# A delta-rule block on one core: output products placed between the products with the inverse, and two element-wise steps given to ScalarE

## The chip, the cores and the metric

The kernel runs on one core of a Trainium2 chip. The metric is the time of one execution on the device in microseconds (us). Before the change the median of 3 runs is 2594.55 us (2590.03 to 2601.16). TensorE does matrix products, VectorE and ScalarE work on rows of elements, GpSimd (POOL in the rows) does small and slow element-wise work, and SyncE (SP) issues DMAs. The engines run beside each other and wait on semaphores.

## The reference

For 2 x 4096 tokens of width 512 the reference adds three things: the input, an attention block and a feed-forward block, both on the layer-normalised input. Cut to what is computed:

```python
xn = layernorm(x)                                   # eps 1e-5
q, k = l2n(heads(xn @ Wq)) * dh**-0.5, l2n(heads(xn @ Wk))   # 16 heads of 32
v, beta = heads(silu(xn @ Wv)), sigmoid(xn @ Wb)
# for each token t, batch and head: S is 32 x 32
#   delta = (v_t - S^T k_t) * beta_t ;  S = S + k_t delta^T ;  o_t = S^T q_t
o = o * rsqrt(mean(o*o) + 1e-5) * o_norm_weight
attn = o @ Wo
ffn = ((silu((xn @ fp8(gate_w)) * gate_scale)) * ((xn @ fp8(up_w)) * up_scale)) @ fp8(down_w) * down_scale
out = x + attn + ffn
```

## The kernel before

**Tiling.** The 4096 tokens of each batch are cut into 16 spans of 256. One span holds both batches: 512 tokens, 4 tiles of 128, and 8 chunks of 32 tokens per batch and head. The recurrence is solved chunk by chunk: for each of 256 problems (2 batches, 16 heads, 8 chunks) a 32 x 32 triangular system is inverted, and the state is then carried over the 8 chunks in turn.

**A span on TensorE**, in the order in which it is issued. (1) Projections: 13 jobs, each a group of 128 output columns, 12 products of 128 x 512 (8 for the beta projection, JOB_B), from the high and low halves of the normalised input and the weights. Between them stand eight groups of Gram products (`gram(g)`, 8 x 4 problems each), K^T K and K^T Q: pairs 0-1 after job 4, 2-3 after job 5, 4 to 7 together after job 8. (2) The output products of the previous span, `project_out(j)` for 4 tiles, 12 products each, jobs 13 to 16. (3) Gate and up products, 24 halves of 8. (4) Eight groups of small products with the inverse (`quads` at L450, the UW products): they give W and U of each problem. Group g writes PSUM bank T[g % 4], so group 4 must wait until group 0 is read. (5) The state chain, 8 chunks c: products with the state, 6 products of the down projection (`down`), then, in some chunks, the transposes of the next span's normalised input (XT_AT), products that update the state, and 6 more down products. All small products are on 32 x 32 tiles of the array and go through the helper `quads` (L306).

**VectorE.** It reads projections, sums squares, reads the Gram results (`read_grams`, L956 transposes them, L958 masks the K^T Q half, L962 multiplies by beta), and solves all systems at once: 62 operations in turn (`row_products` L1020, `off_rows` L1027), each needing the one before. Other work is put between them by operation number: V_AT (transposes of V from PSUM), OUT_AT (`add_out`, adding an output product to the result), VK_AT (`values_by_k`, L1054, one operation that scales V by the norm of k), FUSE_AT (`fuse_tile`: the low part of the last tile, L1003, and gate times up, L1013). `fuse_tile(10)` and `(11)` stand behind the first and second half's transpose of the inverse (`t_transposed`, L1037). After this come `read_w`, the statistics of the next span's input, and in the chain a read, a subtraction, a read and an addition per chunk.

**ScalarE** evacuates projections, computes silu and tanh, makes the high parts, copies U (`copy_u`, L605) and the chain's outputs. **GpSimd** zeroes the matrix of the inverse, does the square roots by Newton steps, and adds the down products. **SyncE** stores a span's result once its four output tiles are added (`wo_added`) and then loads the span after next into the same buffer.

**Order and banks.** Every engine's order is written out by hand. Dense jobs use the PSUM banks D[job % 4]; `take(job)` waits until job - 4 has been read. `tt` holds the transposed inverse with the 32 columns of a problem side by side; it is what TensorE loads as weights in step 4. The output in high and low parts lives in the last four tiles of f_hi and f_lo. The loop's body holds two spans (`two_spans`); two spans stand ahead of the loop, which goes round 7 times.

## Time and profile before

| | |
|---|---|
| median of 3 runs | 2594.55 us |
| profiled execution, its time | 2598.04 us |
| its span, first to last instruction | 2596.3 us |
| mean granted TensorE clock | 0.98 |
| TensorE busy | 2290.9 us, 88% |
| VectorE busy | 1932.2 us, 74% |
| ScalarE busy | 661.6 us, 25% |
| GpSimd busy | 315.2 us, 12% |

The profile is one execution. A line names the engine, the line of the kernel, the operation, the tile written and the tiles read, and how many there are. `128*128` or `32*32` behind an operation on TensorE (PE) is the part of the array; a 32-bit product on a small tile is two instructions, each with its own weight load (PEld). Mean durations of pipelined instructions overlap: what one costs in a row of equals is the distance between starts. A bracket at the end of a line is the idle time of the engine before it and what ended that time; "issue" means that nothing in the profile ended it.

### The profile page before, as it was taken

Reading aid. Unit: us, or ns where it says so; the run is one execution under the profiler, and the core shown is the slowest. Engines: PE = TensorE matmul, PEld = TensorE weight load, DVE = VectorE, ACT = ScalarE, POOL = GpSimd, SP = SyncE. Lnnn points to the kernel's source line nnn. Section 1 sums busy time; section 2 is a strip of 40 time slices with the busy share of each in tenths; the row PEclk is TensorE's granted clock in tenths of the full one; section 3 lists DMA queues with packets and bytes.
Section 4 is the critical chain, followed back from the end, with each engine's and each line's share of the span. In section 5 each row is a group of like instructions: output and inputs, shape, how many; then the busy total and the mean of one; then the engine's idle time right before and its main releaser. Section 6 shows DMA issues by size and latency. Waiting matters only on the chain.

```text
span 2596.3 us, 92717 instructions
## 1 busy us (share of the span) xinstructions
PE 2290.9 (88%) x40736; PEld 1286.9 (50%) x40992; DVE 1932.2 (74%) x3291; ACT 661.6 (25%) x1110; POOL 315.2 (12%) x528
## 2 busy tenths in 40 slices
PE   0198999989899998989989899998989899898996
PEld 0045545455554545455454555545554454545543
DVE  7986685958768596776959587695967769496785
ACT  2123222213222222222222222222222222122221
POOL 4510101001010100102010010201001020100200
PEclk9999999999999999999999999999999999999998
DMA  5100010000001000000000000010100100000010
GB/s 170 61 18 2 3 34 4 33 3 19 18 3 34 3 34 3 17 20 3 34 4 34 3 13 24 3 34 3 34 3 3 34 3 34 4 34 3 2 34 18
DMA packets 27184, 54.56 MB, mean 21 GB/s; under 512 B 5152, under 2 KB 5152, under 8 KB 26784
## 3 DMA queue, kind: packets, MB, share of 16 engines
q1 hardware_dynamic: 26784, 48.55, 5.5%
q8 instruction: 334, 5.47, 0.9%
q14 instruction: 66, 0.54, 0.1%
HBM read 31.76 MB, written 16.78 MB: 19 GB/s over the span
## 4 chain that ended last, share of the span: by engine, by line
PE 88%; issue 6%; DVE 4%; DMA 0%; ACT 0%; POOL 0%; SPq 0%; DVEq 0%
PE D L380 21%; PE T L306 21%; PE D L391 13%; PE D L390 13%; PE D L462 8%; PE D L321 7%; PE D L461 4%; PE D L311 1%; DVE kq L227 1%; DVE at L781 0%; DVE f_lo L780 0%; DVE w_lo L822 0%; DVE stats L744 0%; DVE wgu L233 0%; DVE kq L1042 0%
## 5 line engine op out<-in xcount | busy, mean ns | idle before, releaser
L390 PE MATMUL D<-xt_hi,wgu 128*128 128x512 f16 x1536 | 582.1, 379 | 0.0
L391 PE MATMUL D<-xt_lo,wgu 128*128 128x512 f16 x1536 | 582.1, 379 | 0.0
L462 PE MATMUL D<-wd,f_lo 128*128 128x512 bf16 x768 | 297.0, 387 | 43.1 <-issue 43.1
L380 PE MATMUL D<-xt_hi,w_hi 128*128 128x512 f16 x832 | 319.3, 384 | 12.9 <-issue 12.9
L380 PE MATMUL D<-xt_lo,w_hi 128*128 128x512 f16 x832 | 318.4, 383 | 0.0
L380 PE MATMUL D<-xt_hi,w_lo 128*128 128x512 f16 x768 | 293.9, 383 | 0.0
L598 ACT ACTIVATE sg<-D,gs 128x512 f32<-128x512 f32 x192 | 132.0, 687 | 573.6 <-PE D L391 573.6
L1027 DVE TENSOR_TENSOR at<-at,outer_v 128x62 f32<-128x62 f32 (+15 forms) x496 | 259.3, 523 | 12.1
L1020 DVE TENSOR_TENSOR outer_v<-mt,at 128x62 f32<-128x62 f32 (+15 forms) x496 | 258.2, 521 | 11.6
L391 PEld LDWEIGHTS D<-xt_lo,wgu 128*128 128x128 f16 x1536 | 150.3, 98 | 181.2
L390 PEld LDWEIGHTS D<-xt_hi,wgu 128*128 128x128 f16 x1536 | 150.3, 98 | 181.2
L1113 DVE STREAM_TRANSPOSE outer_p<-T 128x256 f32<-128x256 f32 x128 | 57.6, 450 | 193.4 <-PE T L306 193.4
L461 PE MATMUL D<-wd,f_hi 128*128 128x512 bf16 x512 | 198.2, 387 | 0.0
L306 PE MATMUL T<-kpv,mt 32*32 32x64 f32 x8192 | 136.3, 222 | 67.5 <-issue 67.5
L306 PE MATMUL T<-kq,state 32*32 32x64 f32 x8192 | 155.3, 221 | 24.7 <-ACT kpv L605 18.9
L306 PEld LDWEIGHTS T<-kq,state 32*32 32x32 f32 x8192 | 130.0, 108 | 79.0 <-issue 78.7
L306 PEld LDWEIGHTS T<-kpv,mt 32*32 32x32 f32 x8192 | 126.7, 110 | 81.0 <-issue 81.0
L726 POOL TENSOR_TENSOR rstd<-var_e,neg_half 128x4 f32<-128x4 f32 x16 | 16.4, 1026 | 1222.9 <-DVE var_e L1105 1222.9
L1093 DVE STREAM_TRANSPOSE outer_v<-T 128x256 f32<-128x256 f32 x128 | 57.6, 450 | 143.0 <-PE T L306 143.0
L306 PE MATMUL T<-kpv 32*32 32x64 f32 x8192 | 148.2, 219 | 3.4 <-issue 2.7
L732 POOL TENSOR_TENSOR xs<-xs,fuse 128x512 f32<-128x512 f32 x64 | 81.1, 1267 | 575.8 <-DVE fuse L1087 575.8
L306 PEld LDWEIGHTS T<-kpv 32*32 32x32 f32 x8192 | 125.4, 107 | 46.1 <-issue 45.9
(153 smaller groups left out, 3314.0 us busy)
## 6 DMA issues: line engine op xcount, KB each, us to landing
xs<-_attn_hidden_states_dram SPq DMA_DIRECT2D x34, 512.0 KB, 4.2
out_dram<-xs SPq DMA_DIRECT2D x32, 512.0 KB, 3.3
f_hi<-in_L_ffn_down_w_dram SPq DMA_DIRECT2D x4, 768.0 KB, 4.5
kq<-in_L_ffn_gate_w_dram SPq DMA_DIRECT2D x3, 768.0 KB, 4.4
f_hi<-in_L_ffn_up_w_dram SPq DMA_DIRECT2D x2, 768.0 KB, 6.2
kq<-in_L_ffn_up_w_dram SPq DMA_DIRECT2D x2, 768.0 KB, 6.6
qt<-in_L_attn_Wq_dram SPq DMA_DIRECT2D x1, 1024.0 KB, 8.1
kpv<-in_L_attn_Wk_dram SPq DMA_DIRECT2D x1, 1024.0 KB, 10.4
```

The lines of the kernel that those rows point to most:

```text
L306: last = nc.tensor.matmul(out[s], lhs[s], rhs[s], start=start, stop=True, skip_group_check=shared)
L321: ins = nc.tensor.matmul(D[bank][:, :], o_part[:, m, j * P:(j + 1) * P], w[:, m, :], start=n == 0, stop=n == 3 * MS - 1)
L380: last = nc.tensor.matmul(D[bank][:, :], w[:, k, cols], xp[:, k, :], start=n == 0, stop=n == len(parts) * KT_ - 1)
L390: nc.tensor.matmul(D[bank][:, :], wgu[:, k, c:c + P], xt_hi[:, k, :], start=k == 0, stop=False)
L391: last = nc.tensor.matmul(D[bank][:, :], wgu[:, k, c:c + P], xt_lo[:, k, :], start=False, stop=k == KT_ - 1)
L461: nc.tensor.matmul(D[bank][:, :], f_hi[:, ic, j * P:(j + 1) * P], wd[:, ic, :], start=ic == 0, stop=False)
L462: last = nc.tensor.matmul(D[bank][:, :], f_lo[:, ic, j * P:(j + 1) * P], wd[:, ic, :], start=False, stop=ic == IC - 1)
L598: nc.scalar.activation(sg[:, ic % 2, :], D[bank_of(gate_up_job(2 * ic))][:, :], ACT.Silu, scale=gs[:, ic:ic + 1]).then_inc(sg_ready, 1)
L732: nc.gpsimd.tensor_tensor(xs[:, par, j, :], xs[:, par, j, :], fuse[:, j % 2, :], ALU.add).then_inc(acc_ready, 1)
L1020: solved[0] = step(nc.vector.tensor_tensor(products(j), m_prob[:, :, j, j + 1:].unsqueeze(3).to_broadcast(shape), t_prob[:, :, j, 0:j + 1] ...
L1027: solved[0] = step(nc.vector.tensor_tensor(rest, rest, products(j), ALU.subtract))
L1093: nc.vector.transpose(blocks(outer_v), chain_banks(c)[:, :, :, 0, :]).then_inc(ws_read, 1)
```

## The change

It makes these edits at once.

- **Order on TensorE.** The beta projection moves from job 2 to job 5. Output products of tiles 2 and 3 leave their place before gate-up and become jobs 39 and 40: half a tile (6 products) stands behind inverse groups 1, 3, 5 and 7. Job 8 and the first 4 products of job 9 stand between Gram pairs 4-5 and 6-7.
- **ScalarE.** It masks the K^T Q half of the second 32 problems, 32 calls over one column each, and scales V by the norm of k, 64 calls of 32 elements (8 behind each of the gate silus 2 to 9). VectorE's operations for these two are gone (the mask of the first half stays).
- **VectorE.** All twelve `fuse_tile` stand inside the solve; output additions 2 and 3 move behind inverse reads 4 and 7. The statistics of the next span's input go batch by batch: the first before the chain, the second in chunk 2, with the aggregation in chunks 0 and 3 and the normalisation in chunks 1 and 4; the input's transposes are in chunks 2, 3, 5 and 6. Some steps of the reading stage change their order.
- **Layout.** `tt` keeps the problem number innermost, so that `t_transposed` writes in order and TensorE loads its weights at a step of 32 elements.
- **Buffers.** The normalised output goes into `at` and its high and low parts into the memory of `qt`; f_hi and f_lo are used so by the last span alone. GpSimd zeroes `at` after the low part is made, behind its first Newton steps.
- **Loads and stores** go batch by batch, each with its semaphore.
- **Loop.** Four spans per turn, four ahead of it, 3 turns.

```diff
-JOB_K, JOB_B, JOB_Q, JOB_V, JOB_WO, JOB_GU, JOB_DN = (0, 3, 5, 7), 2, (1, 4, 6, 8), (9, 10, 11, 12), 13, 17, 41
+JOB_K, JOB_B, JOB_Q, JOB_V, JOB_WO, JOB_GU, JOB_DN = (0, 2, 4, 7), 5, (1, 3, 6, 8), (9, 10, 11, 12), (13, 14, 39, 40), 15, 41
-XT_AT = {2: 0, 3: 1, 4: 2, 5: 3}
+XT_AT = {2: 0, 3: 1, 5: 2, 6: 3}
-V_AT = {0: 0, 4: 1, 9: 2, 13: 3}
-OUT_AT = {17: 0, 20: 1, 22: 2, 25: 3}
-VK_AT = 23
-FUSE_AT = {27: 0, 31: 1, 34: 2, 37: 3, 40: 4, 43: 5, 46: 6, 50: 7, 54: 8, 60: 9}
+V_AT = {0: 0, 2: 1, 7: 2, 12: 3}
+OUT_AT = {16: 0, 18: 1}
+VK_AT = {ic: range(8 * (ic - 2), 8 * (ic - 1)) for ic in range(2, 10)}
+FUSE_AT = {20: 0, 24: 1, 27: 2, 30: 3, 33: 4, 36: 5, 39: 6, 42: 7, 45: 8, 49: 9, 53: 10, 58: 11}
+STATS_AT, AGGREGATE_AT, APPLY_AT = {2: 1}, {0: 0, 3: 1}, {1: 0, 4: 1}
...
-        tt = mt[:, :].rearrange("p (n t) -> p n t", t=CHUNK)
+        tt = mt[:, :].rearrange("p (g t n) -> p g t n", g=2, t=CHUNK)
...
-                    project(5)
+                    project(JOB_B)
                     gram(2)
                     gram(3)
                     project(6)
                     project(7)
-                    project(8)
                     gram(4)
                     gram(5)
+                    project(8)
+                    project(9, end=4)
                     gram(6)
                     gram(7)
-                    for job in range(9, PROJECTIONS):
+                    project(9, first=4)
+                    for job in range(10, PROJECTIONS):
                         project(job)
 
                     pe.wait_ge(olo_ready, since(1, 1))
-                    for j in range(TILES):
-                        project_out(j, take(JOB_WO + j))
+                    for j in range(2):
+                        project_out(j, take(JOB_WO[j]))
...
-                            last = quads(T[g % 4][:, 64 * n:64 * n + 64], tt[:, pc, :], kpv[:, 1:3, pc * DH:(pc + 1) * DH])
+                            last = quads(T[g % 4][:, 64 * n:64 * n + 64], tt[:, pc // 32, :, pc % 32], kpv[:, 1:3, pc * DH:(pc + 1) * DH])
                         last.then_inc(tiled_done, 1)
+                        if g % 2:
+                            j, half = 2 + g // 4, g // 2 % 2
+                            bank = bank_of(JOB_WO[j]) if half else take(JOB_WO[j])
+                            project_out(j, bank, groups=range(2 * half, 2 * half + 2))
...
+                    act.wait_ge(m_ready, since(2, 2))
+                    act.wait_ge(q_read, since(1, 1))
+                    for i in range(CHUNK):
+                        masked = nc.scalar.activation(pt[:, 32:64, i], grams[:, :, 1, i], ACT.Identity, scale=causal[:, i:i + 1])
+                    masked.then_inc(p_ready, 1)
...
+                    def values_by_k(n):
+
+                        v_problem = vt[:, n, :]
+                        return nc.scalar.activation(v_problem, v_problem, ACT.Identity, scale=rk[:, n:n + 1])
...
                     for ic in range(IC):
                         silu_gate(ic)
+                        if ic in VK_AT:
+                            if VK_AT[ic][0] == 0:
+                                act.wait_ge(v_ready, since(MS, MS))
+                                act.wait_ge(k_norm_ready, since(1, 1))
+                            for n in VK_AT[ic]:
+                                scaled = values_by_k(n)
...
-                        nc.vector.transpose(tt[:, 32 * s:32 * s + 32, :].rearrange("p n t -> p t n"), t_prob[:, s]).then_inc(tt_ready, 1)
+                        nc.vector.transpose(tt[:, s], t_prob[:, s]).then_inc(tt_ready, 1)
...
                     t_transposed(0)
-                    fuse_tile(10)
                     t_transposed(1)
-                    fuse_tile(11)
-
-                    dve.wait_ge(x_loaded, since(32, 64))
-                    dve.nop(nofuse=True)
+
                     for g in range(8):
                         read_w(g)
                         if g == 1:
                             low_part(IC - 1)
-                        if g > 3:
-                            step(layer_norm_stats(g - 4, 1 - par))
+                        if g == 4:
+                            add_out(2)
+                    read_statistics(0)
+                    add_out(3)
...
-            with dve.Fori(1, SPANS // 2) as it:
-                two_spans(it)
+            with dve.Fori(1, SPANS // TURNS) as it:
+                some_spans(it)
```

## Rows read from the trace of the kernel before

**Rows 1.** The page: the chain that ended last, by engine.

```profile
PE 88%; issue 6%; DVE 4%; DMA 0%; ACT 0%; POOL 0%; SPq 0%; DVEq 0%
```

**Rows 2.** The chain in order of time: start, length (us), engine, tile, line.

```profile
282.89 12.09 PE D L380 x56
...
1040.42 2.16 issue
1042.59 13.94 PE D L380 x56
...
1166.72 0.44 PE D L311 x4
...
1196.32 12.09 PE D L380 x56
...
1222.84 2.68 PE T L306 x178
...
1228.12 10.47 PE D L380 x48
1238.58 10.36 PE D L321 x48
...
2565.95 2.49 DVE sso L1142 x4
```

**Rows 3.** TensorE's timeline, inverse products of two spans: start, us, operation.

```profile
1138.26 2.56 PE L306 MATMUL T<-kpv,mt 32*32 32x64 f32 x168
1142.17 1.98 PE L306 MATMUL T<-kpv,mt 32*32 32x64 f32 x126 [1.36 <-issue]
1146.10 3.59 PE L306 MATMUL T<-kpv,mt 32*32 32x64 f32 x126 [1.95 <-issue]
...
1152.83 0.71 PE L306 MATMUL T<-kq,state 32*32 32x64 f32 x34 [1.19 <-ACT kpv L605]
...
1290.31 3.88 PE L306 MATMUL T<-kpv,mt 32*32 32x64 f32 x261
1296.04 5.47 PE L306 MATMUL T<-kpv,mt 32*32 32x64 f32 x251 [1.85 <-issue]
1302.71 0.21 PE L306 MATMUL T<-kq,state 32*32 32x64 f32 x1 [1.20 <-ACT kpv L605]
```

**Rows 4.** TensorE's timeline in the chain, two half-steps.

```profile
1161.79 1.10 PE L306 MATMUL T<-kpv 32*32 32x64 f32 x64
...
1164.22 1.10 PE L306 MATMUL T<-kq,state 32*32 32x64 f32 x64
```

**Rows 5.** Windows: stretch, length, TensorE busy (matmuls), granted clock, DMA share, GB/s.

```profile
1147.00:1148.00 1.00, 1.00 (x49) 0.50 0.08 16
```

**Rows 6.** VectorE's timeline, from the second half's Gram results to the inverse's transpose.

```profile
1228.17 1.25 DVE L956 STREAM_TRANSPOSE mt<-T 128x1024 f32<-128x1024 f32 x1 [2.35 <-PE T L306]
...
1232.37 0.17 DVE L1020 TENSOR_TENSOR outer_v<-mt,at 128x62 f32<-128x62 f32 x1
...
1247.62 2.29 DVE L1054 TENSOR_TENSOR kpv<-kpv,rk 128x2048 f32<-128x2048 f32 x1
...
1269.86 0.69 DVE L1003 TENSOR_TENSOR f_lo<-fuse,f_hi 128x512 f16<-128x512 f32 x1 [0.23 <-PE D L391]
1270.47 0.74 DVE L1013 SCALAR_TENSOR_TENSOR fuse<-D,usf,sg 128x512 f32<-128x512 f32 x1
...
1283.08 0.28 DVE L1020 TENSOR_TENSOR outer_v<-mt,at 128x120 f32<-128x120 f32 x1
...
1285.45 1.97 DVE L1037 STREAM_TRANSPOSE mt<-at 128x1024 f32<-128x1024 f32 x1
```

**Rows 7.** Groups of ScalarE by line: count, busy us, mean ns, idle before.

```profile
L592 ACT ACTIVATE f_hi<-fuse 128x512 f16<-128x512 f32 x192 | 119.3, 621 | 32.7 <-DVE fuse L1013 32.7
...
L574 ACT ACTIVATE tb<-tb,w_inv 128x64 f32<-128x64 f32 x16 | 5.6, 348 | 26.3 <-DVE tb L923 26.3
...
L616 ACT ACTIVATE wd<-wd,row_inv 128x512 bf16<-128x512 bf16 x12 | 7.4, 706 | 0.0
```

More of the change, by code:

```diff
@@ L312, in transpose_xn, with project_out @@
                 last.then_inc(dense_done, 1)
[L314 to L317 removed]
+            def project_out(j, bank, last=False, groups=range(MS)):
+                hi, lo = (last_hi, last_lo) if last else (o_hi, o_lo)
+                for m in groups:
                     if last:
                         pe.wait_ge(olo_ready, SPANS + m + 1)
[L320 removed]
+                    for n, (o_part, w) in enumerate(((hi, wo_hi), (lo, wo_hi), (hi, wo_lo))):
                         ins = nc.tensor.matmul(D[bank][:, :], o_part[:, m, j * P:(j + 1) * P], w[:, m, :],
[L322 to L324 removed]
+                                                start=m == 0 and n == 0, stop=m == MS - 1 and n == 2)
+                if MS - 1 in groups:
+                    ins.then_inc(dense_done, 1)
             pe.wait_ge(consts, 2)
@@ L370, in take, with project @@
                         return bank_of(job)
-                    def project(job):
-                        bank = take(job)
-                        group = (4, 0, 12, 5, 1, 6, 2, 7, 3, 8, 9, 10, 11)[job]
+                    def project(job, first=0, end=12):
+                        bank = bank_of(job) if first else take(job)
+                        group = (4, 0, 5, 1, 6, 12, 2, 7, 3, 8, 9, 10, 11)[job]
                         cols = slice(group * P, (group + 1) * P)
                         parts = ((w_hi, xt_hi), (w_hi, xt_lo), (w_lo, xt_hi))[:2 if job == JOB_B else 3]
-                        n = 0
-                        for k in range(KT_):
-                            for w, xp in parts:
-                                last = nc.tensor.matmul(D[bank][:, :], w[:, k, cols], xp[:, k, :],
-                                                        start=n == 0, stop=n == len(parts) * KT_ - 1)
-                                n += 1
-                        last.then_inc(dense_done, 1)
+                        products = [(k, w, xp) for k in range(KT_) for w, xp in parts]
+                        for n in range(first, min(end, len(products))):
+                            k, w, xp = products[n]
+                            last = nc.tensor.matmul(D[bank][:, :], w[:, k, cols], xp[:, k, :],
+                                                    start=n == 0, stop=n == len(products) - 1)
+                        if n == len(products) - 1:
+                            last.then_inc(dense_done, 1)
                     def gate_up(half):
@@ L760, in one @@
                 dve.wait_ge(set_v, done[0])
[L763 removed]
+            for b in range(BATCH):
+                dve.wait_ge(x_loaded[b], 16)
             for j in range(TILES):
@@ L980, in two_spans @@
                     k_to_tokens(1)
-                    beta_over_k(0)
-                    o_scale(it, par, after, step)
-                    if first and par == 0:
+                    q_sum(1)
+                    o_scale(it, turn, after, step)
+                    if first and turn == 0:
                         gate_up_scale()
-                    q_sum(1)
-                    read_grams(0)
                     k_sum(2)
+                    b_to_tokens()
                     k_to_tokens(2)
                     o_low()
+                    read_grams(0)
+                    beta_over_k(0)
+                    times_beta(0)
                     q_sum(2)
```

235 lines of the change are left out of this document (127 added, 108 removed).

## The prediction

> **What bounds the kernel now.** I read the page's chain first: 88% of the chain that ended last is TensorE, and another 6% is "issue", time in which the engine waited for nothing that the profile shows [rows 1]. So the span is TensorE's content plus its holes, and the question is where the holes are. The chain in order of time gives the beats [rows 2]: the kernel does 16 spans of tokens, and from the start of the second (282.89) to the end of the sixteenth (2565.95) is 2283.1 us, 152.2 for each of 15. The content of one: 48 output products took 10.36 us, 0.216 each [rows 2]; a group of small products (64 matmul instructions) takes 0.95 us, as 261 of them took 3.88 [rows 3]; in the state chain a half-step of 64 small and 6 dense instructions repeats every 2.43 us [rows 4], which is 0.96 + 1.30 + 0.17 for the crossing between kinds. A span has 392 dense products outside the chain (84.6 us), 16 small groups outside it (15.4), 16 half-steps (38.9) and 4 transposes of 0.44 (1.8) [rows 2]: 140.7 us. So 11.5 us of each span are holes or slow clock.
>
> They lie in four places. (a) The last four groups of Gram products run 1222.84 to 1228.12, 5.3 us for 3.9: 1.4 us. (b) The products with the inverse: 14.6 us from 1138.26 to 1152.83 and 12.4 from 1290.31 to 1302.71 (seven spans are like the one, eight like the other), for a content of 7.7 [rows 3]. The stalls fall inside groups and are "issue": from 1142.17 there are 126 matmuls in 1.98 us and then 1.95 of nothing. I read this as TensorE eating small instructions faster than they arrive: 126 matmuls with their weight loads are 252 instructions in 3.9 us when starved, 65 per us, against 135 per us wanted. The dense work wants 9, so it refills. (c) The chain wants 58 per us, just under the supply, but starts empty; what is left of 11.5 after the rest is about 2.7 us. (d) Back-edges of the loop: 2.2 us idle at 1040.42, then 13.94 us for what takes 12.09 in the next span [rows 2]; there are six of them, and as three show hardly any slow stretch I price one at 3.2 us. The slow stretch is the clock: 0.50 was granted (1.2 GHz of 2.4) in 1147 to 1148 after a 1.95 us stall [rows 5]. At the low level 49 small instructions pass per us; a dense product costs double.
>
> **The change, part by part.**
>
> *Less ahead of the inverse products.* Output products 2 and 3 (24 dense, 5.18 us) leave the stretch between V projections and gate-up. Eight products of the beta projection now stand between Gram pairs 0-3, and 16 dense ones between pairs 4-5 and 6-7. Two pairs at 65 per us of supply then never run dry: hole (a) goes, 1.4, for one more crossing, 0.17. From the start of a span gate-up ended at 94.0 (1290.31 [rows 3] less 1196.32 [rows 2]); now 94.0 - 5.2 - 1.4 + 0.2 = 87.6. For this the first half's read must be in time: an estimate of VectorE's new sequence up to the mask ends at 23.8, and TensorE wants it at 24.1 (60 + 8 + 24 dense products and four groups). I take no stall, with up to 1 us as a bound.
>
> *The tail of the solve.* This is where part of it is lost. All twelve fuse_tile calls stand inside the 62 solve operations now, the last before operation 58. It cannot start before the last gate-up product ends, and TensorE's next work needs the inverse's transpose, which comes behind it. So TensorE stands still for: 0.2 latency, the low part 0.6 (1269.86 to 1270.47), the fused product 0.7, operations 58 to 61 1.1 us (1283.08 to 1285.45 less a low part and a fused product that stood between them), and the transpose, 1.25 [rows 6]. The transpose wrote with a 128-byte step, 1.97 us for 1024 elements; written in place it should cost as the one of Gram results, 1.25. Sum 3.85 us, until 91.5. Before, the first transpose (1285.45) was done when gate-up ended. Is VectorE there in time? The solve ran from 1232.37 to 1285.45, 53.1 us with 4 V transposes less one, 4 output additions, 10 fused tiles, 9 low parts and the scaling of the values (2.2). New: less 2.2 and 1.3 for two additions, plus 2.5 for two more tiles with low parts and 0.6 for the first V transpose; it starts at 34.2 (masking half two on VectorE, 1.2, is gone), which would end it at 87; the products pace it instead. So the tail is real and no longer.
>
> After 3.85 us of idleness the clock will fall as it did after 1.95. Here the price is 0.66 us for the first two groups (128 at 49 per us are 2.6, not 1.9) and up to 1 for dense work: bounds 0 and 1.7, I take 0.8.
>
> *Inverse products with output products between.* 8 groups (7.7) + 24 dense (5.18) + 4 crossings (0.66) = 13.5 us, wanting 1072 instructions; a full buffer had 336 to 522 (the 168 or 261 pairs before the first stall [rows 3]) and 65 per us come in addition, about 880. Enough, so no stalls. Reads by VectorE and copies by ScalarE run under the dense pieces, and the last piece, 1.5 us, hides the last read and copy, where TensorE waited 1.2 before [rows 3]. Chain begins at 91.5 + 13.5 + 0.8 = 105.8; before it was 110.2 (1152.83 less 1042.59) and 106.4.
>
> *Chain.* It starts with about 250 instructions in stock, so I take 1.2 of the 2.7 us of holes (bounds 0.3 and 2.7). Statistics for the second batch move into step 2: with the low part and read_down VectorE is 2.5 us busy, 0.9 late for the next product, which the transpose's 0.44 and 1.3 of dense work just cover; without that cover 0.4 us. Output addition 3 and two statistics (1.9 us) stand ahead of the first read, under that product. The second batch's output additions end at about 106 instead of 56, and SyncE's store and load of that batch are queued behind them; the statistics want the load at about 121, and I take 15 us for a store and a load as enough, at nothing.
>
> *ScalarE.* It takes 32 masking calls of 32 columns and 64 scalings of 32 columns. Its cost per call, bounded by the rows: 64 columns took 0.35 with its wait, and 512 columns 0.62 of which 0.43 are the columns' [rows 7]: 0.17 to 0.35. I take 0.25. Masking: 5 to 11 us, starting at 33 and wanted by the values' silu only, whose results are wanted after 52: hidden. Nothing else of ScalarE is queued behind them until gate-up's first silu at 48. Scaling: 8 per gate-up pair, 1.4 to 2.8 us, where ScalarE has 2.2 of 3.45 free (16 dense products, less a silu and a high part of 0.62 each); at 0.28 it fits. At 0.35 it would be 0.5 late in each of eight pairs, 4 us a span. I take nothing.
>
> *Unrolling by four.* The loop's body holds four spans and four stand ahead of it, so it goes round three times: two back-edges instead of six: 4 x 3.2 = 12.6 us.
>
> *First span.* ScalarE rescales wd for 7.4 us [rows 7] ahead of its first copy, and TensorE's fifth inverse group waits for that copy. Now the standstill (3.8) and two dense pieces stand ahead of that group and cover it: 8 us with the stalls of that span (bounds 3 and 10).
>
> *Strided weights.* The inverse is now stored so that TensorE loads 32 columns at a 128-byte step, 512 loads a span. No row shows TensorE reading so. The nearest is VectorE's write at that step: 0.72 us more for 1024 elements [rows 6], 0.7 ns each, 22 ns a load; four tiles at once and a stream that is paced by instructions (15 ns a pair now) may hide all of it. Bounds 0 and 8192 x 22 ns = 184 us; I take 0, since a pair has 5 ns to spare per tile against what its columns need at 2.4 GHz, 20 per tile of four.
> The Trainium skill speaks against this edit: SBUF — State Buffer, section "Door 1: The DMA port swizzle", says that lines of SBUF are 16 bytes and that each access which crosses into a new line pays a penalty, free steps ending at 4 fp32 values. By it every element of these loads would pay; the transpose's 1.97 against 1.25 us agrees for VectorE's writes, and no row here shows it for TensorE.
>
> **Sum.** A span: 105.8 + 38.9 + 1.8 + 1.2 = 147.7 us, 15 of them and two edges: 2221.8, against 2283.1, a gain of 61.3. With 8 for the first span 69 us off a span of 2596.3: 2527, and with the 1.7 us around it (2598.04) 2529. The profiled execution was 3.5 us above the median of the runs, so a median may come out that much lower.
>
> **Rivals.**
> *Instructions still run dry* (0.17). For it: the 65 per us are an average; the chain wants 58 all the time. Then 1.5 in the chain and 1 in the inverse products come back, 37 us: 2566.
> *Strided weights cost a part* (0.13). If an element took four times as long, a load of 13 ns becomes 53, 20 ns more per four tiles: 128 x 20 ns = 2.6 us a span, 41 us: 2570.
> *Strided weights cost all* (0.08), the slower side. Loads of the four tiles don't overlap: 184 us more, 2713. It decides from 69 us / 8192 = 8.4 ns a load. Against it: loads of 110 ns length pass at 15 ns spacing.
> *The solve becomes the bound* (0.07): the tail or ScalarE's scalings are 4 us later a span, 2593, no change.
> *No slow clock and a full supply in the chain* (0.07): 0.8 and 0.9 us less in each of 16 spans, 27 us: 2502.
> Forecast 0.48. Range 2503 to 2590, the sum's bounds for chain and clock below, the partial rivals above; what is left out is mostly the full strided cost. This kernel's measurement tells 0.5%, 13 us, from no change. Faster 0.78 (the cases under 2581 hold 0.85, less 0.07 for two partial rivals that come together), same 0.11, slower 0.11.
>
> **What would show it.** TensorE idle about 3.9 us before the first inverse product of each span, ended by the inverse's transpose at 1.25 us; inverse products with dense ones in 13.5 to 14.5 us and no mid-group stall; last Gram pairs without stalls; two "issue" gaps of 2.2 us at back-edges; ScalarE's scalings at 0.25 us. Wrong if small products per us fall below 66 in the inverse products at full clock, or if ScalarE's gate silu waits behind scalings.

## The result, and the profile after

The changed kernel took 2602.22 us (median of 20 runs, 2595.02 to 2612.79) against 2594.21 for the kernel before (20 runs): a ratio of 1.003, 95% interval [1.0019, 1.004]. On a second chip it was 2601.68 against 2597.37, 1.0019 [1.0003, 1.0036]. So the time did not change by more than 0.5%, and what little it moved went up. The forecast was 2529, its range 2503 to 2590. The profiled execution took 2603.99 us, its span 2602.3, 75 us over the forecast.

The page of the kernel after, chain that ended last by engine, which answers to [rows 1]:

```profile
PE 89%; DVE 7%; issue 3%; DMA 0%; POOL 0%; ACT 0%; DVEq 0%; SPq 0%
```

"issue" has halved (6% to 3%), as was meant, and VectorE's share has gone from 4% to 7%: a stall on instructions was exchanged for a wait on VectorE. The waits of TensorE name it (line waited for: us in total, times, longest):

```profile
PE T L315 <- DVE mt L1091: 50.5, 12, 4.2
```

They are twelve waits of 4.2 us each, once a span, for the transpose of the inverse. In the first four spans the same pause of 3.9 to 4.0 us is put down to "issue". VectorE's timeline of one span, the seventh, shows what fills it:

```profile
1131.83 0.69 DVE L1057 TENSOR_TENSOR f_lo<-fuse,f_hi 128x512 f16<-128x512 f32 x1
1132.44 0.74 DVE L1067 SCALAR_TENSOR_TENSOR fuse<-D,usf,sg 128x512 f32<-128x512 f32 x1
1133.10 0.27 DVE L1074 TENSOR_TENSOR outer_v<-mt,at 128x120 f32<-128x120 f32 x1
...
1133.98 0.22 DVE L1081 TENSOR_TENSOR at<-at,outer_v 128x62 f32<-128x62 f32 x1
1134.24 2.37 DVE L1091 STREAM_TRANSPOSE mt<-at 128x1024 f32<-128x1024 f32 x2
```

The last fused tile, the last four solve operations and the transpose run one after the other, while TensorE, whose last gate-up product ended at 1131.6, has nothing it may do. TensorE's timeline of the same span (start, us, operation, in brackets the idle time before it), which answers to [rows 3]:

```profile
1131.26 0.38 PE L402 MATMUL D<-xt_lo,wgu 128*128 128x512 f16 x1
1135.83 3.64 PE L315 MATMUL T<-kpv,mt 32*32 32x64 f32 x128 [4.20 <-DVE mt L1091]
1139.41 1.03 PE L330 MATMUL D<-wo_hi,qt 128*128 128x512 f16 x2
...
1142.02 2.10 PE L315 MATMUL T<-kpv,mt 32*32 32x64 f32 x128
1144.06 0.61 PE L330 MATMUL D<-wo_hi,qt 128*128 128x512 f16 x2
...
1145.45 1.76 PE L315 MATMUL T<-kpv,mt 32*32 32x64 f32 x99
...
1150.43 1.16 PE L315 MATMUL T<-kpv,mt 32*32 32x64 f32 x64 [0.32 <-issue]
```

The first 128 small products take 3.58 us (1135.83 to 1139.41), the next 128 take 2.04. The six dense output products between them take 2.61, the next six 1.39. There is no stall inside any of these four pieces: the first two are slow, not interrupted. The last group of the span is interrupted once, for 0.32 us. The windows of this span (stretch, length, TensorE busy with its matmuls, granted clock, DMA share, GB/s), which answer to [rows 5], show why:

```profile
1136.00:1137.00 1.00, 1.00 (x45) 0.50 0.00 0
...
1140.00:1141.00 1.00, 1.00 (x4) 0.50 0.00 0
...
1142.00:1143.00 1.00, 1.00 (x66) 1.00 0.00 0
```

After the pause TensorE is granted 1.2 GHz, not 2.4, for some 6 us of this span, and small and dense products alike cost nearly double.

From the starts of the second to the sixteenth span and of the stretches in them I worked out means for 15 spans (us). The last column is the time at 1.2 GHz in the stretch of the inverse products and in the chain:

| | start to end of gate-up | standstill | inverse stretch | chain to next span | span | at 1.2 GHz in inverse / chain |
|---|---|---|---|---|---|---|
| before | 94.5 | 0 | 13.6 | 44.2 | 152.2 | 1.3 / 3.0 |
| forecast | 87.6 | 3.9 | 14.3 | 41.9 | 147.7 | |
| after | 89.1 | 4.1 | 16.3 | 43.4 | 152.9 | 4.3 / 0 |

The idle time at back-edges lies inside the measured stretches, but not in the forecast's 147.7, which counts two edges apart. So 5.5 us a span were saved ahead of the inverse and 0.8 behind it, and 4.1 and 2.7 were paid between. The balance, 0.7 us a span more (10 us in 15), less the 5 us by which the first span became shorter (159.3 to 154.4), is the 6 us between the two spans (2596.3 and 2602.3), as near as rounded means tell. Of the 16.3 us of the inverse stretch the slow clock took 1.9: in the mean of the 15 spans the first 128 small products and the first six dense ones, the only pieces that meet it, were longer by that than the 2.04 and 1.40 us which such pieces take at 2.4 GHz.

### The profile page after: what moved, and what is told of

Read it like the earlier page. It is cut to its first block, busy times and chain, and to the rows that moved or that the text cites. A ratio compares the mean times of both kernels' runs of the same rounds, so it can differ in the third digit from the quotient of the medians.

```text
span 2602.3 us, 94081 instructions
## 1 busy us (share of the span) xinstructions
PE 2352.2 (90%) x40992; PEld 1293.3 (50%) x40992; DVE 1874.9 (72%) x3275; ACT 968.7 (37%) x2646; POOL 325.3 (13%) x544
## 4 chain that ended last, share of the span: by engine, by line
PE 89%; DVE 7%; issue 3%; DMA 0%; POOL 0%; ACT 0%; DVEq 0%; SPq 0%
PE T L315 22%; PE D L391 21%; PE D L402 13%; PE D L401 13%; PE D L330 7%; PE D L478 7%; PE D L479 6%; PE D L320 1%; DVE kq L233 1%; DVE mt L1091 1%; DVE kpv L1167 1%; DVE at L821 0%; DVE f_lo L820 0%; DVE state L1176 0%; DVE w_lo L862 0%
## 5 line engine op out<-in xcount | busy, mean ns | idle before, releaser
L478 PE MATMUL D<-wd,f_hi 128*128 128x512 bf16 x768 | 293.7, 382 | 1.7 <-issue 1.6
L615 ACT ACTIVATE kpv<-kpv,rk 128x32 f32<-128x32 f32 x1024 | 229.4, 309 | 0.0
L315 PE MATMUL T<-kpv,mt 32*32 32x64 f32 x8192 | 160.6, 238 | 69.7 <-DVE mt L1091 50.5
L766 POOL TENSOR_TENSOR rstd<-var_e,neg_half 128x2 f32<-128x2 f32 x32 | 22.6, 706 | 1487.2 <-DVE var_e L1119 1487.2
L315 PEld LDWEIGHTS T<-kpv,mt 32*32 32x32 f32 x8192 | 148.7, 141 | 101.1 <-issue 100.6
L660 ACT ACTIVATE qt<-T 128x256 f32<-128x256 f32 x128 | 49.2, 384 | 379.3 <-DVE outer_p L1174 379.3
L1096 DVE STREAM_TRANSPOSE kq<-T 128x256 f32<-128x256 f32 x128 | 57.4, 448 | 156.4 <-PE T L315 156.2
L1067 DVE SCALAR_TENSOR_TENSOR fuse<-D,usf,sg 128x512 f32<-128x512 f32 x192 | 143.1, 745 | 26.3 <-PE D L402 26.3
L330 PE MATMUL D<-wo_hi,qt 128*128 128x512 f16 x512 | 160.5, 395 | 1.1 <-issue 1.1
L315 PEld LDWEIGHTS T<-kq,state 32*32 32x32 f32 x8192 | 123.9, 105 | 69.1 <-issue 68.9
```

Of the source, the lines that this page charges most:

```text
L315: last = nc.tensor.matmul(out[s], lhs[s], rhs[s], start=start, stop=True, skip_group_check=shared)
L330: ins = nc.tensor.matmul(D[bank][:, :], o_part[:, m, j * P:(j + 1) * P], w[:, m, :], start=m == 0 and n == 0, stop=m == MS - 1 and n == 2)
L478: nc.tensor.matmul(D[bank][:, :], f_hi[:, ic, j * P:(j + 1) * P], wd[:, ic, :], start=ic == 0, stop=False)
L615: return nc.scalar.activation(v_problem, v_problem, ACT.Identity, scale=rk[:, n:n + 1])
L1067: nc.vector.scalar_tensor_tensor(fuse[:, ic % FUSE_RING, :], D[bank][:, :], usf[:, ic:ic + 1], sg[:, ic % 2, :], ALU.mult, ALU.mult).then_ ...
```

## The experiments

Each comparison is with the kernel before on the same chip; "after" is the changed kernel. The kernel before took 2587.35, 2597.37 and 2590.78 us on the three chips of these runs, so between chips the ratios are compared, not the times.

**Is it the tail?** Theory A: the last fused tiles stand in VectorE's path to the inverse, and the pause makes the clock fall. Its rivals B and C are in the expectation below. A further one, that the small products are slow because of their strided weights, is left to the run on the strided weights. The first run moves both tiles behind the transposes, where they stood before the change.

```diff
-FUSE_AT = {20: 0, 24: 1, 27: 2, 30: 3, 33: 4, 36: 5, 39: 6, 42: 7, 45: 8, 49: 9, 53: 10, 58: 11}
+FUSE_AT = {20: 0, 24: 1, 27: 2, 30: 3, 33: 4, 36: 5, 39: 6, 42: 7, 45: 8, 49: 9}
...
                     t_transposed(0)
+                    fuse_tile(10)
                     t_transposed(1)
+                    fuse_tile(11)
```

> The changed kernel, with fused tiles 10 and 11 behind the first and the second transpose of the inverse, as in the kernel before. Theory A (the standstill ahead of the inverse products is what ate the gain, twice: 4.2 us of idleness and then some 2.8 us because the clock falls to 1.2 GHz behind it): the standstill shrinks to about 1 us, TensorE keeps 2.4 GHz, each span is 5 to 6 us shorter, 16 spans give about 90 us, so about 2510. Theory B (the standstill only fills the instruction supply; without it the same time comes back as stalls inside the small groups): at most 2 us a span, about 2570 to 2600, with issue stalls in the inverse products. Theory C (VectorE is late by itself): the standstill stays above 3 us and the time near 2600.

Measured: 2543.33 us, ratio 0.984 [0.9805, 0.9874]. TensorE's timeline of one span:

```profile
1113.34 2.09 PE L315 MATMUL T<-kpv,mt 32*32 32x64 f32 x128 [1.49 <-DVE mt L1091]
...
1116.76 2.10 PE L315 MATMUL T<-kpv,mt 32*32 32x64 f32 x128
...
1120.19 2.22 PE L315 MATMUL T<-kpv,mt 32*32 32x64 f32 x128
...
1123.74 2.40 PE L315 MATMUL T<-kpv,mt 32*32 32x64 f32 x128
...
1130.26 1.10 PE L315 MATMUL T<-kpv 32*32 32x64 f32 x64
...
1132.69 1.44 PE L315 MATMUL T<-kq,state 32*32 32x64 f32 x64
```

The pause is 1.5 us, the clock falls behind it in none of the 15 spans, and the first 128 products take 2.09 instead of 3.64. A span is 4.0 us shorter. A holds, but its size was too large: 5 to 6 us a span were expected, and the ratio moved by 1.9%, some 49 us (59 between the two traced executions), not 90. The inverse stretch still takes 14.9 us a span where the forecast had 13.5 without slow clock. Its last groups are slower than its first: 2.40 against 2.09 in this span, with no gap that the timeline lists, and in most others with up to 0.6 us of "issue" in a group as well. The stretch without slow clock at 14.9 is only 1.4 us shorter than with it (16.3), though the slow clock costs 1.9: a part, some 0.5 us, came back in the later groups, as theory B has it for the whole. In the chain behind, half-steps of 1.10 us stand beside some of 1.44.

**How long may the pause be?** Only tile 11 moves behind the transpose, tile 10 stays at operation 53.

```diff
-FUSE_AT = {20: 0, 24: 1, 27: 2, 30: 3, 33: 4, 36: 5, 39: 6, 42: 7, 45: 8, 49: 9, 53: 10, 58: 11}
+FUSE_AT = {20: 0, 24: 1, 27: 2, 30: 3, 33: 4, 36: 5, 39: 6, 42: 7, 45: 8, 49: 9, 53: 10}
...
                     t_transposed(0)
+                    fuse_tile(11)
                     t_transposed(1)
```

> The changed kernel, with only fused tile 11 moved behind the first transpose; tile 10 stays inside the solve. A middle dose. Theory A: a standstill of about 2.6 us; if the clock falls as it does after 4.2 us, the gain is the 1.6 us alone, 26 us, about 2575; if it does not fall after so short a pause, 1.6 + 2.8 a span, 70 us, about 2530. Theory B: no gain, 2590 to 2600. Theory C: standstill as before, 2600.

Measured: 2568.9, ratio 0.9933 [0.9911, 0.9953]. Its waits (line waited for: us in total, times, longest):

```profile
PE T L315 <- DVE mt L1091: 33.9, 12, 2.9
```

The pause is 2.8 us, and the clock falls behind it in nine of the 15 spans, a case that the expectation didn't hold. The gain over the kernel after is 1.0%, 25 us, what was expected of the shorter pause alone; the inverse stretch became only 0.7 us shorter (15.5 for 16.3). Three lengths of the same pause thus give three answers: 1.5 us never, 2.8 in nine of 15, 4.2 always.

**The unrolling.** Two spans per turn instead of four, six back-edges instead of two.

```diff
-TURNS = 4
+TURNS = 2
```

> The changed kernel with two spans per turn of the loop instead of four, seven turns: six back-edges instead of two. If a back-edge costs the 3.2 us that I gave it, 13 us more, about 2615. Rival: unrolling by four also placed the instruction stream so that the third span of each turn stalls 3.4 us in the Gram products; two spans per turn lay the stream otherwise, and the time is 2595 to 2605 with the stalls elsewhere or gone.

Measured: 2605.67, ratio 1.0074 [1.0049, 1.0099], 0.44% or 11 us more than the kernel after, and by the two intervals anything from 4 to 18 us. Four back-edges were priced at 12.6 us. The run agrees but does not isolate them, since other terms moved too. In the traces TensorE is idle 1.9 to 2.4 us at each back-edge of either kernel, which is some 9 us for four, and no slow clock follows it in either. The Gram stalls of the 7th, 11th and 15th span are gone in this kernel, which gives back about as much. The chains that end in a back-edge take 46.3 us, 3.5 more than the others, so more than the back-edge lies in them: "issue" stalls inside their small products.

**The strided weights.** The old layout is put back: the transpose writes at a 128-byte step again, and TensorE loads 32 adjacent columns.

```diff
-        tt = mt[:, :].rearrange("p (g t n) -> p g t n", g=2, t=CHUNK)
+        tt = mt[:, :].rearrange("p (n t) -> p n t", t=CHUNK)
...
-                            last = quads(T[g % 4][:, 64 * n:64 * n + 64], tt[:, pc // 32, :, pc % 32], kpv[:, 1:3, pc * DH:(pc + 1) * DH])
+                            last = quads(T[g % 4][:, 64 * n:64 * n + 64], tt[:, pc, :], kpv[:, 1:3, pc * DH:(pc + 1) * DH])
...
-                        nc.vector.transpose(tt[:, s], t_prob[:, s]).then_inc(tt_ready, 1)
+                        nc.vector.transpose(tt[:, 32 * s:32 * s + 32, :].rearrange("p n t -> p t n"), t_prob[:, s]).then_inc(tt_ready, 1)
```

> The changed kernel with the transposed inverse stored as before (32 columns of a problem side by side, VectorE's transpose writing at a 128-byte step). If TensorE loads strided weights at no cost (128 small products and their loads took 1.96 us at 2.4 GHz, 1.90 before), the groups keep their time, and only the standstill grows by 0.7 us with the transpose: about 12 us more, 2614. If strided loads cost, the groups get faster than 1.9 us per 128 and the kernel does not lose: 2590 to 2602.

Measured: 2606.48, ratio 1.0086 [1.0053, 1.012]. TensorE's timeline of one span:

```profile
1136.56 3.63 PE L315 MATMUL T<-kpv,mt 32*32 32x64 f32 x128 [4.87 <-DVE mt L1091]
...
1142.71 2.00 PE L315 MATMUL T<-kpv,mt 32*32 32x64 f32 x128
1144.64 0.60 PE L330 MATMUL D<-wo_hi,qt 128*128 128x512 f16 x2
```

The first group is as slow as with strided weights (3.63 against 3.64), so the strided weights aren't the cause. At 2.4 GHz 128 products take 1.93 us from start to start (1142.71 to 1144.64) against 2.04 strided: the stride costs 0.11 per 128, 0.4 us a span, some 7 us in all. The transpose in place gives back 0.7 (the pause is 4.87, not 4.20). By these two figures the new layout gains 0.3 us a span, 5 us in all; the ratios (1.0086 against 1.003) say 15, with intervals that almost touch, so the sign holds and the size is open.

**The kernel after again.** It shares the chip with the next three runs.

> The changed kernel itself, to stand beside the others of this set on one chip. All theories: 1.003 times the kernel before.

Measured: 2601.68, ratio 1.0019 [1.0003, 1.0036].

**The rest of the pause.** On the edit of the first run, the ten fused tiles inside the solve are placed a few operations later, so that VectorE doesn't wait there for products.

```diff
-FUSE_AT = {20: 0, 24: 1, 27: 2, 30: 3, 33: 4, 36: 5, 39: 6, 42: 7, 45: 8, 49: 9}
+FUSE_AT = {22: 0, 26: 1, 29: 2, 32: 3, 35: 4, 38: 5, 41: 6, 45: 7, 49: 8, 54: 9}
```

> The version with fused tiles 10 and 11 behind the transposes, whose first fused tile now waits behind two more solve operations (22 instead of 20, the later ones likewise), where VectorE had stood idle 1.7 us for the first gate-up pair. If the rest of the standstill (1.5 us) is VectorE's busy time, it shrinks to 0.2 us and the kernel gains 1.3 x 16, 21 us on the 2543 of that version: ratio to before about 0.976. Rival: TensorE uses those 1.5 us to fill up on instructions, and half or more comes back as stalls in the inverse products: 0.98 to 0.984.

Measured: 2526.09, ratio 0.9734 [0.9706, 0.9762]. VectorE's transpose in one span, then TensorE's timeline of the same:

```profile
1103.11 1.25 DVE L1091 STREAM_TRANSPOSE mt<-at 128x1024 f32<-128x1024 f32 x1
```

```profile
1104.87 0.38 PE L402 MATMUL D<-xt_lo,wgu 128*128 128x512 f16 x1
1105.17 2.10 PE L315 MATMUL T<-kpv,mt 32*32 32x64 f32 x128
1107.20 0.60 PE L330 MATMUL D<-wo_hi,qt 128*128 128x512 f16 x2
```

The inverse is ready 0.5 us before the last gate-up product starts, and TensorE goes on without a pause. A span takes 147.3 us. Between the kernel after and this one, on the same chip, lie 2601.68 less 2526.09, 75.6 us, or 5.6 us a span by the traces (152.9 less 147.3). They differ only in where twelve VectorE steps stand. The inverse stretch takes 15.0 us without a pause ahead of it and without slow clock, still 1.5 more than the forecast's 13.5.

**Output products back in their old place**, on the first run's edit: all four tiles stand ahead of gate-up, nothing between the inverse groups. The ten fused tiles inside the solve go back to their old operations with them, since gate-up comes later.

```diff
-JOB_K, JOB_B, JOB_Q, JOB_V, JOB_WO, JOB_GU, JOB_DN = (0, 2, 4, 7), 5, (1, 3, 6, 8), (9, 10, 11, 12), (13, 14, 39, 40), 15, 41
+JOB_K, JOB_B, JOB_Q, JOB_V, JOB_WO, JOB_GU, JOB_DN = (0, 2, 4, 7), 5, (1, 3, 6, 8), (9, 10, 11, 12), (13, 14, 15, 16), 17, 41
...
-OUT_AT = {16: 0, 18: 1}
+OUT_AT = {16: 0, 18: 1, 21: 2, 24: 3}
...
-FUSE_AT = {20: 0, 24: 1, 27: 2, 30: 3, 33: 4, 36: 5, 39: 6, 42: 7, 45: 8, 49: 9}
+FUSE_AT = {27: 0, 31: 1, 34: 2, 37: 3, 40: 4, 43: 5, 46: 6, 50: 7, 54: 8, 60: 9}
...
-                        if g % 2:
-                            j, half = 2 + g // 4, g // 2 % 2
-                            bank = bank_of(JOB_WO[j]) if half else take(JOB_WO[j])
-                            project_out(j, bank, groups=range(2 * half, 2 * half + 2))
...
```

> The version with fused tiles 10 and 11 behind the transposes, and all four output products back in one block before gate-up. It leaves the other edits (ScalarE's share, Gram order, layout, unrolling). Theory: interleaving is worth what the starved small products lost, as the inverse products go back to some 13.5 us with mid-group stalls and slow clock, and the chain gets slow clock again, less the 1.5 us of standstill: 2.5 to 4 us a span, ratio to before 0.998 to 1.01. Rival: the dense pieces only moved the stalls, the small products take what the supply gives wherever they stand: ratio 0.98 to 0.99.

Measured: 2607.7, ratio 1.0047 [1.0026, 1.0068]. TensorE's timeline of one span:

```profile
1138.32 3.02 PE L315 MATMUL T<-kpv,mt 32*32 32x64 f32 x190
...
1146.92 2.26 PE L315 MATMUL T<-kpv,mt 32*32 32x64 f32 x126 [1.35 <-issue]
1150.56 1.38 PE L315 MATMUL T<-kpv,mt 32*32 32x64 f32 x70 [1.38 <-issue]
1153.11 1.93 PE L315 MATMUL T<-kq,state 32*32 32x64 f32 x64 [1.17 <-ACT kpv L628]
```

The stalls of [rows 3] are back, again behind about 126 products: TensorE is idle 5.8 us a span between its first inverse product and the chain, 1.2 of them the wait for ScalarE's last copy. In the kernel after 0.3 us of such idle time is left. The chain's slow clock is back as well (2.9 us a span). Against the first run the interleaving is worth 2.1% (1.0047 less 0.984), 54 us. But the first run has a pause of 1.5 us ahead of the inverse products and this one has none. Against the run before, which has no pause either and ran on the same chip, it is 3.1%, 82 us; the places of the fused tiles differ there too.

**ScalarE's share given back to VectorE**, on the first run's edit: the second mask, and the scaling of the values at operation 23.

```diff
-                    for i in range(CHUNK):
-                        masked = nc.scalar.activation(pt[:, 32:64, i], grams[:, :, 1, i], ACT.Identity, scale=causal[:, i:i + 1])
...
-                            for n in VK_AT[ic]:
-                                scaled = values_by_k(n)
...
+                        if op == 23:
+                            nc.vector.tensor_tensor(vt[:, :, :], vt[:, :, :], per_token(rk), ALU.mult).then_inc(vk_ready, 1)
```

> The version with fused tiles 10 and 11 behind the transposes, with the second mask and the scaling of the values back on VectorE (one operation each, 1.2 and 2.2 us). Theory: VectorE's solve sets the standstill, 1.7 us of it is absorbed where it was idle, so the standstill goes from 1.5 to about 3.2 us and the clock falls in half of the spans: 1.7 + 1 us a span, ratio to before about 1.00. Rival: VectorE has more room than that, and giving work to ScalarE bought nothing: 0.984.

Measured: 2560.1, ratio 0.9872 [0.9847, 0.9896]. That was a miss: I expected it near the kernel before, and it is 0.3% behind the first run, with intervals that overlap. The first run's VectorE timeline has an idle stretch ahead of the first fused tile that could have taken up the 3.4 us of added work (1.2 and 2.2); the second line is the same place in this run:

```profile
1074.06 0.75 DVE L1067 SCALAR_TENSOR_TENSOR fuse<-D,usf,sg 128x512 f32<-128x512 f32 x1 [1.68 <-PE D L402]
```

```profile
1079.16 0.75 DVE L1054 SCALAR_TENSOR_TENSOR fuse<-D,usf,sg 128x512 f32<-128x512 f32 x1 [1.68 <-PE D L402]
```

It did not: the wait is as long with the added work, which stands behind it. What shrank are smaller waits inside the solve, ahead of the first transpose of V and of later fused tiles; VectorE's idle time there fell from 4.0 to 2.3 us a span. The pause before the inverse products grew only from 1.5 to 1.9 us. Behind this 1.9 us the clock fell in three of the 15 spans, a fourth point beside the three above.

**No back-edge at all**, on the kernel with the tiles later: eight spans per turn, eight ahead of the loop, so it goes round once.

```diff
-TURNS = 4
+TURNS = 8
```

> The version with the later fused tiles (0.973 of the kernel before), unrolled by eight: the loop goes round once, no back-edge is left. Theory: two back-edges fewer at about 3 us each, 6 us, ratio about 0.971, unless the stalls in the Gram products (3.2 us in three spans now) move: then 0.968 to 0.976.

Measured: 2512.84, ratio 0.9702 [0.9681, 0.9724]. It is the fastest kernel of this study, 3.0% under the kernel before. The step from 0.9734 is 0.3%, some 8 us where 6 were expected, and the two intervals overlap; in the trace the idle time at back-edges is gone.

**Moving the instructions.** In the kernel after, stalls of 3.2 to 3.9 us a span remain in the Gram products of the 7th, 11th and 15th span and, in the first four, of the 2nd. TensorE's timeline of its 7th span:

```profile
1063.95 1.88 PE L315 MATMUL T<-kq 32*32 32x64 f32 x118
1067.63 0.38 PE L315 MATMUL T<-kq 32*32 32x64 f32 x10 [1.80 <-issue]
1071.50 1.65 PE L315 MATMUL T<-kq 32*32 32x64 f32 x100
1074.78 0.64 PE L315 MATMUL T<-kq 32*32 32x64 f32 x28 [1.62 <-issue]
```

In the kernel with the tiles later they are 3.0 to 3.2 us, in the same spans and behind the same products. The question was whether they hang on the place in the instruction stream. First I put 128 TensorE nops ahead of projection 7 in each third span of four.

```diff
                     project(6)
+                    if turn == 2:
+                        for n in range(128):
+                            pe.nop(nofuse=True)
                     project(7)
```

> The version with the later fused tiles, with 128 empty instructions of TensorE between projections 6 and 7 in the third span of each four: they compute nothing and only shift where the instruction stream is cut. Theory (the 3.2 us of stalls in the Gram products of spans 6, 10 and 14 come from where blocks of 252 instructions end): the stalls of these spans change or go although TensorE has more to do; 128 empty instructions cost 1 to 3 us in each of four spans, so the time stays within 6 us, ratio 0.972 to 0.976. Rival (the stalls have to do with that span's data or waits): they stay at 3.2 us and the kernel is 4 to 12 us slower, 0.975 to 0.978.

Measured: 2515.98, ratio 0.9714 [0.9691, 0.9737]. TensorE's timeline without the nops, then with them:

```profile
1036.15 1.88 PE L315 MATMUL T<-kq 32*32 32x64 f32 x118
...
1039.28 0.38 PE L315 MATMUL T<-kq 32*32 32x64 f32 x10 [1.25 <-issue]
```

```profile
1033.83 1.88 PE L315 MATMUL T<-kq 32*32 32x64 f32 x118
...
1037.24 0.38 PE L315 MATMUL T<-kq 32*32 32x64 f32 x10 [1.53 <-issue]
```

The stall stands behind the same 118 products. Taken at its word that is the rival's outcome, but the profile doesn't count the nops, and whether they reach the stream in the form written I can't show, so this run settles nothing. The next kernel, also on the one with the tiles later, repeats 32 products of 128 columns at the same place (64 instructions with their loads; the sums in PSUM start anew behind them).

```diff
+                        if turn == 2 and job == 7:
+                            for n in range(32):
+                                nc.tensor.matmul(D[bank][:, 0:128], w_hi[:, 0, cols], xt_hi[:, 0, 0:128], start=True, stop=True)
```

> The version with the later fused tiles, with 32 products of 128 columns (64 instructions with their loads) repeated ahead of projection 7 in the third span of each four; they are overwritten, and cost some 2 us in each of four spans. The empty instructions of the run before did not show in the instruction count, so this is the shift with real ones. Theory (blocks of about 252 instructions, and a stall where one ends inside small products): in spans 6, 10 and 14 the stall that stood behind 118 of 128 small products comes 32 products earlier, behind about 86, or moves out of the Gram products; in other spans of the turn stalls move too. Rival (bound to this place for another reason): the stall stays behind 118.

Measured: 2536.33, run once, against 2581.42. TensorE's timeline of the same Gram products:

```profile
1039.47 2.07 PE L315 MATMUL T<-kq 32*32 32x64 f32 x128
...
1045.03 2.00 PE L315 MATMUL T<-kq 32*32 32x64 f32 x128
```

The stalls of the 7th, 11th and 15th span are gone. Others appeared in the Gram products of the 6th, 10th and 14th (3.2 to 3.4 us), here the 6th, and ahead of a projection product in the 8th, 12th and 16th (1.0 to 1.3):

```profile
892.62 0.32 PE L315 MATMUL T<-kq 32*32 32x64 f32 x9 [1.53 <-issue]
...
899.98 0.63 PE L315 MATMUL T<-kq 32*32 32x64 f32 x27 [1.90 <-issue]
```

In the spans with the repeated products these could also have given the instructions time to arrive. That doesn't explain the new stalls in the spans without them, which in the loop's body lie ahead of the added code and are shifted only by the copy ahead of the loop. So, as far as one execution shows, the stalls do hang on where the code lies, though they didn't move by the number of products that I had expected.

## Why the prediction was wrong, point by point

**What was read rightly.** The four places of lost time were real. The tail of VectorE's solve was found and sized at 3.85 us; it was 4.2, and the 0.35 more is the time from the end of the transpose to the first product, which I had left out. Output products between the inverse groups end nearly all of the stalls there (5.8 us of idle time a span without them, 0.3 with them). Two back-edges instead of six are worth some 9 us by their idle time, where 12.6 stood. ScalarE's masking (0.17 us a call) and scaling (0.21) cost less than the 0.25 estimated and stay hidden. The strided weights cost 7 us of the 0 to 184 given.

**The sum of the miss.** Forecast against measured, per span: end of gate-up 87.6 to 89.1 (1.5), standstill 0.3, inverse stretch 2.0, chain 1.5, together 5.2 before rounding. In 15 spans that is 78 us, less the 6.4 that the forecast held for two back-edges apart, and 3.1 for the first span (151.3 forecast, 154.4 measured): 75 us. (Of the two kinds of spans that I counted before the change, eight are of the long kind and seven of the short, not the other way round; the 152.2 doesn't depend on it.)

**The step that failed is that the small products would run without stalls and at their full rate, because a mean supply of 65 instructions per us was enough.** It stands in three terms: "Two pairs at 65 per us of supply then never run dry: hole (a) goes"; "Enough, so no stalls" for the inverse products, 13.5 us; and 1.2 us for the chain. The runs showed in their place 1.5, 0.8 and 1.5 us more a span, 3.8 of the 5.2, some 57 us of the 78; the chain's part is not all for want of instructions.

*End of gate-up.* In spans without a stall it is 87.7, as forecast. Hole (a) is gone in eleven of the 15. In the other four Gram stalls remain and make them 3.7 to 4.4 us longer, 1.1 in the mean; shorter waits ahead of a projection product in the 6th, 10th and 14th span are the other 0.2. Stalls that move with the place of the code show that the supply isn't a mean.

*Inverse products.* Of the 16.3 us, 1.9 are the slow clock. The other 14.3 stand against 13.5. A group of 128 takes 2.04 us undisturbed where the content had 1.92, dense pieces included that is 13.8; the third and the fourth 128 are slower, 2.14 and 2.42 us in the mean of 15 spans, with 0.3 us idle on "issue". Without any slow clock the stretch took 14.9 and 15.0 us in two of the runs.

*Chain.* It holds 2.7 us beside its content of 40.7, with 1.2 taken. The slow clock of 3.0 us a span, which had cost about 1.5, left it. By the trace there stay 0.9 us of "issue" inside small products, 0.3 at back-edges, 0.6 in chunks 3 and 7, mostly waits for VectorE, and 1.1 in groups of 64 that are slow at 2.4 GHz with nothing idle, 1.44 us for instance instead of 1.10 [rows 4]. (The last figure is an estimate, their time from start to start less the 1.03 us of an undisturbed one.) Such groups were in the kernel before too, about 0.9 us a span by the same estimate, and the rows that I chose did not show one. Here one stands at a granted clock of 1.00:

```profile
1000.78 1.48 PE L306 MATMUL T<-kpv 32*32 32x64 f32 x64
```

One of after (from 1158.13) lies beside transfers that take 71 to 90% of the DMA engines, another (from 1163.32, 1.34 us) beside none. What slows them isn't settled.

**A second step, the price of the clock behind the standstill, was mis-sized.** I wrote 0.66 us for the first two groups, from "49 small instructions per us" [rows 5], plus part of a microsecond for dense work, 0.8 in all. A window's count takes in the products that overlap its edges, which is too many for a window of 1 us: the one of after shows 45 where 128 products in 3.58 us are 36 per us. A row that I had quoted had the right figure: 126 products in 3.59 us [rows 3], 35 per us. By that row 128 products are 3.6 us, and the excess is 1.6, not 0.66. I also let the low clock end after the first two groups or so, and in some spans six dense products behind them lost another 1.2 us. So 2.7 us were lost in the span shown and 1.9 in the mean, where 0.8 stood and 1.7 was the upper bound. That is 1.1 a span, 17 us of the 78.

The runs price the standstill and its clock together without such readings. Taking them away gave 5.6 us a span (152.9 to 147.3); the forecast had them at 3.85 and 0.8, 4.7. The difference, 0.9 us a span or 14 us, is what the miss owes to the standstill. So the standstill is why the change gained nothing, but most of its cost was in the forecast; it accounts for less than a fifth of what the forecast missed.

**Among the rivals** the outcome lies nearest to the one that made the solve the bound (2593, no change), with a chance of 0.07. That VectorE's tail stands ahead of the inverse was in the forecast itself, and the solve did not take the rival's 4 us more. The rival with dry instructions (2566) is the one whose mechanism came true: it had 1.5 us in the chain and 1 in the inverse products, and 1.5 and 0.8 were measured. It had no Gram stalls, and it stood alone, while slow clock and Gram stalls came on top. Without the standstill the rest of the change was worth what I had forecast for all of it: 2526 measured, 2529 forecast. That agreement is chance, since the forecast contained a standstill with 4.7 us a span and missed some 4 us elsewhere.

The Trainium skill, TensorE: Matmul & The Clock Gate, section "HAM oscillation — how this bites in real kernels", describes a kernel in which a wait inside every tile sends the clock down anew, so that each next tile starts cold. The trace agrees for pauses of 4.2 us (always) and not for those of 1.5 us (in none of 15 spans). The prediction had the clock falling too; what it had wrong was how much slow work follows.

## What to carry to other kernels

A mean rate says whether instructions suffice over a stretch, not whether a stall falls inside it. When a forecast puts stalls at nothing because the mean is enough, give that term a price and a chance: here three such terms made 57 us. When a change makes TensorE wait once per tile, price the wait with what follows at half clock, and take that price from rows of the same work at the low clock, from start to start, never from a window's count. Here a wait of 4.2 us a span, with slow work behind it, cost 75 us in all, what the rest of the change had earned. On the engine that feeds the stretch, put work that nobody waits for behind the result that TensorE waits for: moving two fused tiles behind that result, and ten others back by two to five operations, turned no gain into 2.7%.

## What the runs showed of the hardware

- Whether TensorE's clock falls behind a pause goes with the length of the pause, in the same place of the kernel: 1.5 us in none of 15 spans, 1.9 in three, 2.8 in nine, 4.2 and 4.9 in every one, there with 2.7 to 6.1 us at 1.2 GHz in the inverse products.
- TensorE's weight loads of 32 fp32 values at a 128-byte step cost 0.11 us more per 128 products (2.04 against 1.93), while VectorE's transpose with writes at that step took 1.97 us for 1.25 [rows 6]. The Trainium skill, SBUF — State Buffer, section "Door 1: The DMA port swizzle", has a penalty for each new 16-byte line; the runs show it small for these loads.
- Stalls of 3.2 us a span, which the profile puts down to "issue", left three spans and came up in three others (3.2 to 3.4) when 64 more instructions stood at one place of the code (one execution). A kernel with an edit elsewhere may gain or lose such microseconds unasked.
- A back-edge of the loop left TensorE idle for 1.9 to 2.4 us in most kernels. In the two with instructions added at one place it was more (2.9 us at one of two with the nops, 3.7 and 3.2 with the 64), so its price also hangs on where the code lies. The kernel that goes round once has no such idle time.
- Undoing an offload of 3.4 us a span cost 0.3%, within the noise, where the relieved engine had 4.0 us of idle time of its own ahead of the result that TensorE waits for.
